# A three-layer CIN on Trainium2: three more split tiles, one more hi slot and one more product slot, and gathers spread over GpSimd's tiles

## The reference

```python
x0 = xk = inputs                                   # [samples, 39, 16]
for idx, (W, b) in enumerate(params):              # W: [39, fields of xk, 128]
    z = jnp.einsum('bhd,bkd,hks->bsd', x0, xk, W) + b[None, :, None]
    z = jax.nn.relu(z)
    if idx != n_layers - 1:
        xk = z[:, :64, :]
        direct.append(z[:, 64:, :])
    else:
        direct.append(z)
logit = jnp.sum(jnp.concatenate(direct, axis=1), axis=-1)
```

## Time and profile before

| | |
|---|---|
| median of 3 runs | 1244.64 us (1243.7 to 1245.4) |
| the profiled execution | 1244.94 us |
| its span | 1243.1 us |
| TensorE busy | 1179.9 us, 95% (3856 matmuls) |
| VectorE busy | 1061.9 us, 85% |
| GpSimd busy | 1002.6 us, 81% |
| ScalarE busy | 580.7 us, 47% |
| granted TensorE clock | 0.999 |

### The profile page before, as it was taken

How to read it: one execution, slowest core, us unless ns; L and a number is a source line. 1 busy time by engine, 2 the same in 40 slices (tenths; PEclk the granted TensorE clock), 3 DMA queues, 4 the chain that set the end, 5 groups by cost and what they waited for, 6 DMA issues and landing times.

```text
span 1243.1 us, 14868 instructions
## 1 busy us (share of the span) xinstructions
PE 1179.9 (95%) x3856; PEld 726.5 (58%) x3856; DVE 1061.9 (85%) x927; ACT 580.7 (47%) x563; POOL 1002.6 (81%) x629
## 2 busy tenths in 40 slices
PE   0289999999999999999999999999999999999999
PEld 0155666656565665656566565656656565666665
DVE  2278998989899898989889898998989898998984
ACT  1145444444545444454544445454444545444545
POOL 6678897998889899888989888888988889765651
PEclk9999999999999999999999999999999999999999
DMA  4785726365472626556262745637274563627000
GB/s 125 242 256 191 223 63 218 125 182 201 157 226 60 218 108 206 177 172 211 84 204 97 225 159 172 211 102 215 79 233 140 172 211 123 212 72 231 9 1 1
DMA packets 110269, 196.21 MB, mean 158 GB/s; under 512 B 52975, under 2 KB 64334, under 8 KB 110249
## 3 DMA queue, kind: packets, MB, share of 16 engines
q1 hardware_dynamic: 100009, 193.33, 47.2%
q0 software_dynamic: 10240, 2.64, 2.0%
HBM read 193.36 MB, written 12.78 MB: 166 GB/s over the span
## 4 chain that ended last, share of the span: by engine, by line
PE 69%; POOL 13%; DVE 8%; issue 6%; ACT 2%; DMA 2%; POOLq 0%; SPq 0%; DVEq 0%; ACTq 0%
PE acc L845 67%; POOL lo L464 7%; POOL emb L454 6%; DVE prod L706 3%; DVE lo L719 2%; ACT hi L556 2%; DVE acc L706 1%; DVE hi L716 1%; DMA x_tiles<-x_rows 0%; DMA x_rows<-x_rows 0%; DVE xk L706 0%; PE acc L925 0%; POOLq L163 0%; DMA x_rows<-emb 0%; ACT xk L522 0%
## 5 line engine op out<-in xcount | busy, mean ns | idle before, releaser
L706 DVE TENSOR_TENSOR prod<-x_tiles,xk 128x1024 f32<-128x1024 f32 (+2 forms) x643 | 757.5, 1215 | 123.9 <-PE acc L845 83.4
L464 POOL TENSOR_TENSOR lo<-prod,hi 128x1024 fp32r<-128x1024 f32 (+1 forms) x288 | 690.5, 2400 | 141.1 <-ACT hi L556 136.4
L845 PE MATMUL acc<-prod,wfull 128*128 128x512 f32 (+2 forms) x1408 | 660.6, 593 | 0.0
L556 ACT ACTIVATE hi<-prod 128x1024 fp32r<-128x1024 f32 (+1 forms) x291 | 308.4, 1060 | 406.3 <-DVE prod L706 322.4
L845 PE MATMUL acc<-hi,whi 128*128 128x512 f32 (+1 forms) x800 | 353.0, 441 | 57.7 <-ACT hi L556 57.6
L845 PEld LDWEIGHTS acc<-prod,wfull 128*128 128x128 f32 (+2 forms) x1408 | 266.8, 189 | 205.7 <-issue 177.4
L454 POOL DMA_INDIRECT emb<-table,block_idx x320 | 308.6, 964 | 69.3 <-issue 63.9
L845 PE MATMUL acc<-lo,whi 128*128 128x512 f32 (+1 forms) x736 | 316.1, 517 | 2.4 <-POOL lo L464 1.2
L845 PE MATMUL acc<-hi,wlo 128*128 128x512 f32 (+1 forms) x800 | 316.1, 395 | 0.0
L845 PEld LDWEIGHTS acc<-hi,whi 128*128 128x128 f32 (+1 forms) x800 | 150.9, 189 | 112.4 <-issue 72.2
L845 PEld LDWEIGHTS acc<-lo,whi 128*128 128x128 f32 (+1 forms) x736 | 138.3, 190 | 133.2 <-issue 104.0
(11 more groups left out here) (72 smaller groups left out, 163.4 us busy)
## 6 DMA issues: line engine op xcount, KB each, us to landing
x_tiles<-x_rows SPq DMA_DIRECT2D x304, 512.0 KB, 5.1
x_rows<-x_rows SPq DMA_DIRECT2D x16, 624.0 KB
x_tiles<-x_rows SPq DMA_DIRECT2D x32, 256.0 KB, 5.6
x_stack<-x_rows SPq DMA_DIRECT2D x48, 156.0 KB
emb<-table,block_idx POOLq DMA_INDIRECT x320, 3.8
x_rows<-emb SPq DMA_DIRECT2D x16, 152.0 KB, 3.3
x_tiles<-w SPq DMA_DIRECT2D x1, 768.0 KB, 6.1
x_tiles<-w SPq DMA_DIRECT2D x1, 704.0 KB, 8.6
```

Of the source, the lines that this page charges most:

```text
L464: nc.gpsimd.tensor_tensor(lo[0:r, product_slot(j), :], prod[0:r, product_slot(j), :], hi[0:r, part_slot(j), :].bitcast(f32), ALU.subtract) ...
L556: nc.scalar.activation(hi[0:r, part_slot(j), :], held(n, parity, j)[0:r, :], ACT.Copy).then_inc(hi_ready, 1)
L706: nc.vector.tensor_tensor(held(n, parity, j)[0:r, :], in0, in1, ALU.mult).then_inc(product_ready, 1)
L845: mm = nc.tensor.matmul(z[:, c], w[0:r], part[0:r, c], start=first and i == 0, stop=last and i == len(weights) - 1)
```

## The change

KINDS gets new tables: three F tiles of a step become D, and the letters are placed anew. A step has 19 F, 18 G, 8 D and 2 H: layer 0 3 G and 4 F (before 2 and 5), layer 1 7 G, 5 D, 7 F (before 8, 3, 8), layer 2 8 G, 3 D, 8 F (before 8, 2, 9). There are seven product slots and five hi slots. A hi slot that held a G tile counts as free once TensorE has done its hi part (new semaphore hi_used, on the last matmul of that part) and GpSimd its lo; for D and H tiles it stays with tile_used. In layer 2 gathers lie behind all G tiles. SyncE waits for the gathered rows behind tile 12 of layer 2 instead of tile 9.

```diff
-KINDS = ["GFFGFFF", "GFDGF" * 2 + "GFHGF" + "GFDGF", "GFFGF" + "GFFGD" + "GFHGF" + "GFDGF"]
+KINDS = ["GFGFGFF", "GFDGFDGFDGFGHGFDGFDF", "GFGFGFGFGDGFHGFDGFDF"]
...
-PRODS, PARTS = 6, 4
+PRODS, PARTS = 7, 5
...
+        hi_used = sem("hi_used")
...
-            WRITE_AFTER = 9
+            WRITE_AFTER = REST - 1
...
-                between = max(1, len(tiles) - (4 if l == 2 else 0))
+                between = len(tiles)
...
-                            act.wait_ge(tile_used, reached(n, parts_before(n, j), "FDGH"))
+                            before = parts_before(n, j)
+                            if KIND[before] == "G":
+                                act.wait_ge(hi_used, reached(n, before, "G"))
+                                act.wait_ge(lo_ready_g, reached(n, before, "G"))
+                            else:
+                                act.wait_ge(tile_used, reached(n, before, "FDGH"))
...
-                            multiply(j, [whi[:, w, :], wlo[:, w, :]], hi[:, part_slot(j), :], j == start, False)
+                            mm = multiply(j, [whi[:, w, :], wlo[:, w, :]], hi[:, part_slot(j), :], j == start, False)
+                            if KIND[j] == "G":
+                                mm.then_inc(hi_used, 1)
```

## The result

The changed kernel takes **1277.51 us** (median of 6 runs, 1277.35 to 1280.27), the kernel before, run beside it, 1245.23 (1243.70 to 1246.18). The ratio is 1.0266, with a 95% interval of [1.0253, 1.0279]: 2.7% slower. The profiled execution took 1277.4 us with a span of 1275.6, at a granted clock of 0.999.

What follows compares the result with a forecast made beforehand. Bound: a loop of waits from TensorE's slots through VectorE, ScalarE and GpSimd back, 74.1 us against 71.87 a block. First block +4.2, 13 periods +28.9, last two blocks +0.9, +0.4, +1.0: +35.4, 1280 us; range 1254 to 1292.

Steps and rivals of the forecast that it cites:

- The loop: TensorE frees slots, VectorE does layer 1, ScalarE makes hi, GpSimd makes lo, TensorE waits: 74.1 us a block.
- The inner loop: VectorE's own loop with TensorE, by way of the subtraction of 1.18, without GpSimd: 72.5 us a block.
- The stall before lo 1.18: TensorE waits about 1.6 us because VectorE does that subtraction only behind the reduction and product 0.0.
- The 0.21 behind one's own subtraction: On VectorE, a product waiting for its predecessor's subtraction starts 0.21 us later; four such waits in layer 1, 0.83 us.
- Rival 3: VectorE's products in a run start 1.22 us apart, not 1.13: +1.1 us a block, 1295 us; chance 3%.
- TensorE's prices: Matmul time per tile: F 1.72 us, G or D 1.39, H 0.93; unstalled block 71.58, with the change 70.6.
- Does the larger pool give a head start? Not here.: Seven product slots give VectorE no lead at layer 1's start: products 1.0 to 1.4 still wait five tiles back.
- the wrap: Where slot numbers run on into the next block: 47 tiles modulo 7 leave 5, as modulo 6 did.
- The sum, +35.4: Whole kernel against the profiled execution: first block +4.2 (prologue's +1.8 included), 13 periods +28.9, last two blocks +0.9, +0.4, +1.0.
- Rival 1: GpSimd keeps up and only VectorE's loop stands, 72.5 us a block: 1258 us; chance 13%.
- Rival 2: Faster: seven product slots hold the lead over the wrap, TensorE bounds at 70.6 us a block: 1229 us; chance 12%.
- Theory C: From the experiments' expectations: VectorE simply has too much work a block, wherever that work stands; no chance given.

Runs made afterwards that it cites:

- slots in rounds: Changed kernel with its seven product slots dealt out in rounds of 7, 7, 7, 7, 6, 6, 7 tiles a block: 1283.33 us, ratio 1.0312 to the kernel before.

## Why the prediction was right

By its own steps, with the forecast of 1280.0 against 1277.5:

- **The loop.** 12.57 + 0.32 against 12.86 measured, 29.65 against 29.69, 10.16 against 10.20, 21.35 against 21.30, 0.04 against 0.05; 74.1 against 74.09. In VectorE's leg two errors of some 0.3 met, and that is luck. The prediction took the waits of before from their brackets (0.62 and 0.71); by the distances between starts (725.79 to 727.61, 733.27 to 735.20, less 1.13 each) they were 0.69 and 0.80. With a pair of products that took 0.1 longer than a pair in a run (2.44 for 2.35, at 741.11) that is most of why, in the changed kernel, the leg's work is 29.40 and not 29.65. The rest is the 0.29 for which product 0.0 waits for the copy of the stack, a wait that the prediction did not have. Each leg was cut by itself: VectorE's by 2.3 gave 2.4 a block, GpSimd's gave 1.7 and brought out the inner loop, ScalarE's by 1.1 gave 0.7, down to where GpSimd's own two lo hold lo 0.4.
- **The inner loop,** 72.5: 72.39 once the long one was cut.
- **The stall before lo 1.18,** "about 1.6": 1.65 in the row's bracket; the rest comes by lo 2.8, as said.
- **The 0.21 behind one's own subtraction,** from one row: 1.33 to 1.35 for 1.13 at all four places. Rival 3, products in a run at 1.22 each, gave 1295; the time and the distances of 1.13 and 1.33 speak against it. The rule behind it, of the Trainium skill, "VectorE: DVE Perf Modes", section "The DRAIN you can't avoid", is that the next operation starts only when the pipe is empty and that a semaphore between costs nothing extra. The 1.13 fits only the exception that the section makes for operations that are not held; the 0.21 at a wait doesn't fit what it says of the semaphore.
- **TensorE's prices.** 71.58 without stalls: 71.47 with the old tables; an F made D 0.35 for 0.33. The 70.6 for the new tables no run reached.
- **"Does the larger pool give a head start? Not here."** Right in its result (the kernel with old slots takes the same time). Its reason, the wrap, is only half of it: with the wrap repaired nothing was gained either, because the product that waits for lo 2.8 then leads the run.
- **Hi slots and hi_used at nothing:** right, as far as the run with the old slots shows them together. **SyncE at nothing:** right; VectorE waits for no tile load in the loop, and ScalarE's copy of the stack begins right behind hi 1.18.
- **A slip in the working:** the loop of before is said to have five spacings from lo 0.0 to the late lo 2.10. There are six; 748.12 + 6 x 4.76 + 0.4 + 2.38 gives the 779.5 that stands there.
- **The sum, +35.4,** was 2.9 too high against the profiled execution (+32.5). The first block: its lo are spaced as worked out (51.00 to 61.78, 10.78 for 10.76), but the first came 1.8 earlier than before, not at the same time, so the prologue's +1.8 didn't appear. That is luck too: VectorE's first product waits for the first loads, and they were there 1.8 earlier (48.60 for 50.43). In the runs of this study the first lo stands anywhere from 49.90 to 52.83:

```profile
51.00 2.38 POOL L465 TENSOR_TENSOR lo<-prod,hi 117x1024 fp32r<-117x1024 f32 x1 [3.25 <-ACT hi L562]
...
61.78 2.36 POOL L465 TENSOR_TENSOR lo<-prod,hi 117x1024 fp32r<-117x1024 f32 x1
```

Lo 2.8 of block 0 then stands at 131.37 on TensorE, not 133.16. The 13 periods are 963.24 for 963.3:

```profile
131.37 0.73 PE L851 MATMUL acc<-lo,whi 128*128 128x512 f32 x2 [0.99 <-POOL lo L465]
...
1094.61 0.73 PE L851 MATMUL acc<-lo,whi 128*128 128x512 f32 x2 [0.99 <-POOL lo L465]
```

The last two blocks came 1.0 under their terms (from 1094.61 to the end 181.0, worked out as 182.0). There, too, two errors partly cancel. Up to TensorE's first wait in the perceptron (1215.50, before 1181.53) it took 120.9 from lo 2.8; before it took 114.5 from lo 2.10, and 3.69 lie between the two, so this is +2.7 where block 14 and block 15's layer 1 had been given +1.3. From there to the end it is 60.1 for 61.6, -1.5 where the slower subtractions had been given +1.0: TensorE waits for no lo in that stretch, so they weren't on the path. Part of the 2.7 is a wait of TensorE for a lo of GpSimd in block 15's layer 1 (1.03 in the bracket at 1201.47), which had no term; the rest I didn't follow up.

- **The rivals.** Rival 1 is what the kernel does with two gathers moved (1255 for 1258). Rival 2 asked for the slots to hold the lead over the wrap; they don't by themselves, and with eight slots the time is 1243, not 1229. Theory C, a plain excess of VectorE work, had the number right for the slots in rounds, but the moved gathers took 1.7 us a block off and eight slots 2.4, with all of that work left in.

The three added D tiles would save TensorE 1.0 us a block. They put 1.9 us more work on VectorE's leg (29.40 for 27.54), where waits of 1.5 were all there was to spare, took ScalarE's hi 0.4 behind three activations, and one more lo into layer 0 on GpSimd. With the loop at 74.1, the 70.6 that TensorE needs no longer counted.

## What to carry to other kernels

When the busiest engine reads 95% or more and the next 85%, follow one buffer around before giving work from the first to the second: the legs from slot to slot, through each engine's own order, must sum to less than the period. An instruction on a half-idle engine can cost its length in such a loop, up to where the next loop takes over (here 0.7 of 1.1 us). A reserve of slots was worth no more here than the distance at the worst place: seven slots gave nothing, with the wrap repaired or not, and eight gave 2.4 us a block. A cut in one loop has to be checked in the others, since work moved out of one can land in the next. And move one unit of work, not three: here the first D paid 0.35 us a block, and the next, at the one place tried, cost 0.4.

## What the runs showed of the hardware

In the last block nothing is held in PSUM, so VectorE's subtraction and GpSimd's both read two operands in SBUF. The term of +1.0 rested on two rows; the timeline after shows how the two get in each other's way. VectorE, then GpSimd:

```profile
1232.65 2.78 DVE L725 TENSOR_TENSOR lo<-prod,hi 128x1024 fp32r<-128x1024 f32 x1
...
1238.98 1.22 DVE L722 TENSOR_TENSOR hi<-prod,hi 64x1024 fp32r<-64x1024 f32 x1
```

```profile
1232.00 2.36 POOL L465 TENSOR_TENSOR lo<-prod,hi 128x1024 fp32r<-128x1024 f32 x1 [0.47 <-ACT hi L562]
1238.99 3.48 POOL L465 TENSOR_TENSOR lo<-prod,hi 128x1024 fp32r<-128x1024 f32 x1 [4.63 <-ACT hi L562]
```

Where GpSimd was first (1232.00 to 1234.36), VectorE's subtraction ends at 1235.43, about 1.1 behind it; where VectorE was first, at 1238.98, GpSimd's takes 1.1 longer (3.48 for 2.38). Two later subtractions of VectorE, which met no GpSimd operation in progress, took 1.22 and 1.23; GpSimd's third one, which came 0.12 behind the first of these, took 3.37. In each of these meetings the one that comes second waits, whichever engine it is. The Trainium skill, "SBUF — State Buffer", section "Who interferes with whom", says so: a VectorE instruction with two SBUF inputs contends with a GpSimd one that reads SBUF, the shared port pair is an exclusive lock, and issue order decides who waits. The trace agrees. It would also explain what the held products buy: with the product in PSUM the subtraction at 741.50 above lasts 1.21, and GpSimd's lo that begins beside it at 741.70 keeps its 2.40. No run here took the holding away to measure it, and by the account above none of this was on TensorE's path in the last block.
